# Multiplying node states in pairs with seven half products in a three-layer GNN kernel

## What is computed

```python
def first_block(x, Ws_self, Ws_neigh, bs, src, dst):
    deg = segment_sum(ones, dst, n); inv_deg = 1 / clip(deg, 1)
    h = x
    for l in range(3):
        neigh = segment_sum(h[src], dst, n) * inv_deg
        h = h @ Ws_self[l] + neigh @ Ws_neigh[l] + bs[l]
        if l != 2:
            h = relu(h)
    return h
x = layernorm(x + first_block(x, ...))
x = layernorm(x + messages(x, ...))       # 25 tiles of gathered messages
```

## Time and profile before

| | |
|---|---|
| device time, median of 3 executions | 1868.69 us (1867.55 to 1871.56) |
| span of the profiled execution | 1942.4 us |
| first aggregate starts | 227 us |
| first state of layer 1 multiplied (k = 2) | 252 us |
| y of the last aggregate | 1466 us |

### The profile page before, as it was taken

How to read it: one execution, slowest core, us unless ns; L and a number is a source line. 1 busy time by engine, 2 the same in 40 slices (tenths; PEclk the granted TensorE clock), 3 DMA queues, 4 the chain that set the end, 5 groups by cost and what they waited for, 6 DMA issues and landing times.

```text
span 1942.4 us, 23120 instructions
## 1 busy us (share of the span) xinstructions
PE 1847.2 (95%) x7910; PEld 1133.5 (58%) x7910; DVE 1175.3 (61%) x1955; ACT 623.7 (32%) x1432; POOL 1137.9 (59%) x1087
## 2 busy tenths in 40 slices
PE   8999999999999989999999999999997699999987
PEld 4455555554555545555555556666665477777765
DVE  6866778677444433444344436555535489899977
ACT  1566532332000000000000000111115478788875
POOL 4400000364888877888788822777776667677770
PEclk9999999999999989999999999999998799999998
DMA  5365665433555344544444443566644234344340
GB/s 163 123 210 174 222 206 180 128 102 95 142 145 139 105 128 116 145 124 132 108 132 124 121 130 128 197 210 198 209 157 117 71 96 114 105 109 114 110 109 26
DMA packets 239540, 265.35 MB, mean 137 GB/s; under 512 B 130757, under 2 KB 176527, under 8 KB 239420
## 3 DMA queue, kind: packets, MB, share of 16 engines
q1 hardware_dynamic: 204028, 205.79, 34.7%
q0 software_dynamic: 34480, 57.58, 10.9%
q10 hardware_dynamic: 912, 0.46, 0.1%
HBM read 174.44 MB, written 89.27 MB: 136 GB/s over the span
## 4 chain that ended last, share of the span: by engine, by line
PE 70%; DVE 11%; issue 6%; ACT 4%; another core or an unknown queue 3%; POOL 3%; DMA 2%; SPq 0%; DVEq 0%; POOLq 0%; ACTq 0%
PE low L1228 37%; PE mid L1054 23%; PE low L1258 3%; PE top L1085 2%; DVE table L2023 1%; PE mid L1239 1%; ACT table L1491 1%; DVE sort L1831 1%; PE mid L1069 1%; DVE table L2026 1%; POOL sort L900 1%; POOL table L922 1%; DVE table L2040 1%; DVE wbuf L2002 1%
## 5 line engine op out<-in xcount | busy, mean ns | idle before, releaser
L1228 PE MATMUL low<-table,abuf 125*125 125x512 f16 x3750 | 844.0, 382 | 7.3 <-issue 7.2
L1228 PEld LDWEIGHTS low<-table,abuf 125*125 125x125 bf16 x3750 | 508.3, 137 | 315.2 <-issue 43.4
L1054 PE MATMUL mid<-wbuf,h_t 128*125 128x512 f32 x1200 | 556.5, 601 | 5.8 <-DVE st_out L1759 5.1
L917 POOL DMA_INDIRECT by_src<-scat_row,sort x416 | 487.1, 1171 | 126.1 <-issue 120.8
L922 POOL DMA_INDIRECT table<-msg_table,wbuf x270 | 294.3, 1090 | 128.3 <-issue 85.2
L1054 PEld LDWEIGHTS mid<-wbuf,h_t 128*125 128x125 f32 x1200 | 215.4, 189 | 217.3 <-issue 202.5
L1769 DVE SCALAR_TENSOR_TENSOR y<-low,inv_deg,st_in 125x512 f32<-125x512 f32 x75 | 56.1, 749 | 462.1 <-PE low L1228 309.7
L1713 DVE TENSOR_TENSOR abuf<-abuf,row_scale 125x750 bf16<-125x750 bf16 (+6 forms) x156 | 265.9, 1719 | 0.8
L949 POOL DMA_INDIRECT sort<-msg_table,sort x180 | 193.2, 1073 | 92.2 <-issue 54.5
L1258 PE MATMUL low<-table,wbuf 128*125 128x256 f32 x900 | 212.7, 387 | 18.1 <-ACT table L1491 11.2
L900 POOL TENSOR_TENSOR sort<-sort 128x416 f32<-128x416 f32 x26 | 31.9, 1226 | 320.7 <-DVE sort L1831 320.7
(11 more groups left out here) (245 smaller groups left out, 1595.8 us busy)
## 6 DMA issues: line engine op xcount, KB each, us to landing
abuf<-adj SPq DMA_DIRECT2D x75, 781.2 KB
adj<-table SPq DMA_DIRECT2D x25, 781.2 KB, 4.6
states<-st_out SPq DMA_DIRECT2D x75, 256.0 KB
st_in<-states SPq DMA_DIRECT2D x75, 256.0 KB
flips<-y_flip SPq DMA_DIRECT2D x48, 256.0 KB
h_t<-flips SPq DMA_DIRECT2D x192, 64.0 KB
early_rows<-sort POOLq DMA_DIRECT2D x35, 320.0 KB
table<-early_rows SPq DMA_DIRECT2D x24, 448.0 KB
```

Of the source, the lines that this page charges most:

```text
L917: pool.indirect_dma_start(out=by_src, out_offset=bass.IndirectOffsetOnAxis(ap=place_i[:, k * PIECE + j:k * PIECE + j + 1], axis=0), in_=sc ...
L1054: last = pe.matmul(to[0:TN, :], h_t[i % 2][:, k, 0:TN], weights[l % 2][:, a, k, :], start=k == 0, stop=k == KC - 1)
L1228: last = pe.matmul(p_agg[k % 2][0:TN, :], a_tile[k % 3][:, a, :], table[ps % 2][0:TN, a, h, :], start=a == 0 and h == 0, stop=a == TILES - ...
```

## The change

In layers one and two the first 22 states of a layer (`PAIRED`) are multiplied two at a time. State r (even tile) and q = r + 1 are stacked as a 2x2 matrix of half blocks (upper and lower 256 features), the two weight matrices as another, and the product is made of seven half products in place of eight; a half product is two matmuls. For that DVE forms sums and differences of the weights once a layer (`mix_weights`, in k = 1 and k = 26, into the other weight buffer), of the states once a pair (`mix_states`), and puts the half products together (`unmix_*`). A pair is begun in an odd k of layer one (four half products at a == 6) and ended in the next (three at a == 2); in layer two it is begun in an even k. `mix_states` stands at the end of DVE's work of the aggregate before the pair is begun. States 47 to 49 and 72 to 74 are multiplied as before. `h_t` has four buffers, and all four banks of `p_mid` hold half products. Because `mix_weights` needs the other weight buffer, the weights of layer 2 are loaded in k = 25. Two scratch tiles of the sort move into another buffer, so ACT's bin masks wait for `s_count` (the end of `bin_starts`) in place of `s_tot`.

```diff
+    def pair_begun(k):
+        r = k + PAIRED
+        return [r] if k < 2 * TILES and 3 <= k % TILES <= PAIRED + 1 and k % TILES % 2 else []
+    def pair_ended(k):
+        return pair_begun(k - 1) if k else []
...
-                if k == 2:
-                    sp.wait_ge(s_ps, TILES)
+                if k == TILES:
+                    sp.wait_ge(s_pn, TILES + PAIRED)
+                    sp.wait_ge(s_ps, TILES + PAIRED)
                     for a in range(2):
                         load_weights(2, a)
...
+            def pair_first(r):
+                q, l, n = r + 1, r // TILES, pair_number(r)
...
+                pe.wait_ge(s_row, r)
+                pair_product(p_pair[0], h_t[q % HT][:, 0:HALF, :], upper).then_inc(s_half, 1)
+                pe.wait_ge(s_mixed, 1 + n + 1)
+                wm = weights[(l + 1) % 2]
+                pair_product(p_pair[1], mixed[:, 1, :, :], wm[:, 0, HALF:KC, :]).then_inc(s_half, 1)
+                pe.wait_ge(s_own, r)
+                pair_product(p_pair[2], mixed[:, 0, :, :], wm[:, 0, 0:HALF, :]).then_inc(s_half, 1)
+                pair_product(p_pair[3], h_t[r % HT][:, 0:HALF, :], wm[:, 1, 0:HALF, :]).then_inc(s_ps, 1)
+            def pair_second(r):
...
+                pe.wait_ge(s_own, r + 1)
+                pair_product(p_pair[3], h_t[r % HT][:, HALF:KC, :], wm[:, 1, HALF:KC, :], False).then_inc(s_pn, 1)
+                pair_product(p_pair[0], h_t[q % HT][:, HALF:KC, :], w[:, 0, HALF:KC, :], False).then_inc(s_pn, 1)
+                pair_product(p_pair[2], mixed[:, 2, :, :], w[:, 1, HALF:KC, :], False).then_inc(s_ps, 1)
...
+            def copy_first(r):
...
+                act.activation(st_out[(r + 1) % 2][0:TN, :], p_pair[0][0:TN, :], ACT.Copy).then_inc(s_half, 1)
...
+            def mix_weights(l):
...
+                ch.link(dve.tensor_tensor(to[:, 0, 0:HALF, :], w[:, 1, 0:HALF, :], w[:, 0, 0:HALF, :], ALU.subtract))
+                ch.link(dve.tensor_tensor(to[:, 0, HALF:KC, :], w[:, 1, HALF:KC, :], to[:, 0, 0:HALF, :], ALU.subtract))
+                dve.tensor_tensor(to[:, 1, 0:HALF, :], w[:, 1, HALF:KC, :], w[:, 1, 0:HALF, :], ALU.subtract)
+                dve.tensor_tensor(to[:, 1, HALF:KC, :], w[:, 0, HALF:KC, :], to[:, 0, HALF:KC, :], ALU.subtract).then_inc(s_wmix, 1)
+            def mix_states(r):
...
+                ch.link(dve.tensor_tensor(s1, upper_r, lower_r, ALU.add))
+                dve.tensor_tensor(upper_r, upper_q, upper_r, ALU.subtract)
+                ch.link(dve.tensor_tensor(s2, s1, upper_q, ALU.subtract))
+                dve.tensor_tensor(s4, lower_q, s2, ALU.subtract).then_inc(s_mixed, 1)
+            def unmix_first(r):
...
+                ch.link(dve.tensor_tensor(common, common, p_pair[1][0:TN, :], ALU.add))
...
+                dve.tensor_tensor(p_pair[2][0:TN, :], p_pair[2][0:TN, :], bias[0:TN, r // TILES, :], ALU.add)
...
+                ch.link(dve.tensor_tensor(st_out[r % 2][0:TN, :], common, p_pair[3][0:TN, :], ALU.add))
+                dve.tensor_tensor(st_out[r % 2][0:TN, :], st_out[r % 2][0:TN, :], p_pair[2][0:TN, :], ALU.add).then_inc(s_own, 1)
+            def unmix_rows(r):
...
+                ch.link(dve.tensor_tensor(p_pair[3][0:TN, :], st_out[(r + 1) % 2][0:TN, :], p_pair[3][0:TN, :], ALU.add))
+            def unmix_second(q):
...
+                dve.tensor_tensor(st_out[q % 2][0:TN, :], st_out[q % 2][0:TN, :], p_pair[2][0:TN, :], ALU.add).then_inc(s_own, 1)
...
+                for one in pair_begun(k):
+                    unmix_first(one)
+                for one in pair_ended(k):
+                    unmix_rows(one)
+                    for i in (one, one + 1):
+                        row_scales(i)
+                        row_lo(i)
+                    unmix_second(one + 1)
...
+                if k in (1, TILES + 1):
+                    mix_weights(k // TILES + 1)
...
+                for one in pair_begun(k + 1):
+                    mix_states(one)
```

More of the change, by code:

```diff
@@ L144, in gnn_kernel @@
     y_flip = sb("y_flip", [P, D])
-    h_t = [sb(f"h_t{b}", [P, KC, P]) for b in range(2)]
+    h_t = [sb(f"h_t{b}", [P, KC, P]) for b in range(HT)]
+    mixed = sb("mixed", [P, 3, KC // 2, TN])
+    deg_row = mixed[0:TILES, 0, 0, :]
     row_max = sb("row_max", [P, 1])
@@ L312, in gnn_kernel @@
     p_s = p_mid[:, 3 * D:4 * D]
+    p_pair = [p_mid[:, b * D:(b + 1) * D] for b in range(4)]
     p_b = [p_top[:, 0:D], p_top[:, D:2 * D]]
@@ L517, in made_at, with paired, pair_ended_last, pair_number @@
         return [n for n in (i - 1,) if by_dma(n)] + [n for n in (i,) if TILES <= n < AGGS and not by_dma(n)]
+    def paired(i):
+        return TILES <= i < AGGS and i % TILES < PAIRED
+    def pair_begun(k):
[3 more added lines that the diff above has]
+        return pair_begun(k - 1) if k else []
+    def pair_ended_last(k):
+        return bool(pair_ended(k)) and first_tile(k + 1)
+    def pair_number(r):
+        l, t = divmod(r, TILES)
+        return (l - 1) * (PAIRED // 2) + t // 2
+    def rows_bank(i):
+        if paired(i):
+            return p_pair[3] if i % TILES % 2 == 0 else p_pair[0]
+        return p_n[i % 2]
+    def singles_at(k):
+        return [i for i in made_at(k) if not paired(i)]
+    def stored_at(k):
+        return pair_begun(k) + [r + 1 for r in pair_ended(k)] + singles_at(k)
     def flips_loaded(n):
@@ L782, in _ @@
                 if not first_tile(k):
-                    for i in made_at(k):
+                    for i in stored_at(k):
                         store_state(i)
@@ L1194, in _ @@
                 for a in range(TILES):
-                    for state in made_at(k):
+                    for r in pair_ended(k):
+                        if a == 2:
+                            pair_second(r)
+                    for r in pair_begun(k):
+                        if a == 6:
+                            pair_first(r)
+                    for state in singles_at(k):
                         if a == 6 and not by_dma(state):
                             transpose_y(state)
-                        if a == (2 if by_dma(state) else 12):
+                        if a == (12 if not by_dma(state) else 2 if first_tile(k) else 14):
                             product(state, 0)
@@ L1444, in _ @@
                 bin_masks(bins_first(k))
-                for state in made_at(k):
+                for r in pair_begun(k):
+                    copy_first(r)
+                for r in pair_ended(k):
+                    row_hi(r)
+                    row_hi(r + 1)
+                for state in singles_at(k):
                     if not by_dma(state):
@@ L1939, in _ @@
                     one_hot_rows(builder_of(TILES + k + 1))
-                if k + 1 < AGGS:
+                if k + 1 < AGGS and not pair_ended_last(k):
                     scale(k + 1, 0)
```

85 lines of the change are left out of this document (61 added, 24 removed).

## The result

The changed kernel is slower: 1878.76 us median (1878.13 to 1881.31, 4 runs) against 1868.78 us (1867.55 to 1871.56, 4 runs), ratio 1.0053, 95% interval [1.0039, 1.0067]. That is +10.0 us where -2.2 were forecast. That it lies inside is luck: the part that was given 0.48, 1862 to 1872, missed, and the cause is not one that the sum held.

The account below looks back on a forecast made before the run. PE bounds k = 14 to 49, DVE's chain k = 1 to 13. Terms +16.7 - 1.7 - 18.9 + 1.7 = -2.2 us give 1868.7 - 2.2 = 1866.5 us; range 1853 to 1879.

Parts of the forecast that it names:

- the part that was given 0.48: Whole kernel: the forecast itself, a time of 1862 to 1872 us, with chance 0.48.
- PE's saving: Each pair on PE: 14 matmuls in place of 16, 1.72 us; 37.8 us for 22 pairs if nothing else waits.
- Prices of DVE's instructions: DVE's added work: `unmix_first` 2.64 us, four sums of `mix_states` 1.66 us, `mix_weights` 4.8 us.
- y of k = 13 at 498.1: DVE's chain in k = 1 to 13: grows by 15.4 us, from 482.73 to 498.1 us.
- passes 3, 4, 5: -0.7, +5.1, -0.9: DVE's stretches from y of k-1 to y of k, for k = 3, 4, 5: changes in us.
- k = 15 at 513.2: PE ends aggregate 14 at 513.2 us, against 496.5 before: 16.7 us late.
- The load that is moved: Layer 2's weights going out in k = 25 cost 0 to 5 us; 1.7 taken together with the clock.
- rival 2: Loads of k = 25 too late for `mix_weights`: aggregate 28 waits, clock falls, +4.4 us, 1873; chance 0.16.
- Rival 3: POOL's scatter becomes the bound, up to 21 us late against 17 us of room: +6 us, 1875; chance 0.09.
- The sum along PE: PE's path: +16.7 up to aggregate 14's end, -1.7 layer one, -18.9 layer two, +1.7 moved load and clock: -2.2 us.
- Rival 3's own price: During POOL's scatter: 16 `mix_states` of 1.66 us hold POOL as well, ending it up to 26.6 us later.

Follow-up runs that it names:

- e7: The changed kernel with DVE's sums of layer one done on one column instead of all: 1859.5 us, ratio 0.9945.
- e9: The changed kernel with ACT's copy of a pair's first half product in k = 3 and 5 behind the second of seven evictions: 1874.9 us, ratio 1.0027.
- e10: The changed kernel with layer two's weights loaded one aggregate sooner, in k = 24: 1880.7 us, ratio 1.0055.
- clean trace: A second trace of the unchanged kernel, no edit: span 1866.0 us, time 1867.85 us.

## Why the prediction was wrong, step by step

- **PE's saving** (1.72 us a pair, 17.66 and 15.95 in turn): right to 0.01 us.
- **Prices of DVE's instructions**: right. `unmix_first` took 2.65 us (2.64), `mix_states` 1.57 (1.66), `mix_weights` 4.83 (4.8).
- **y of k = 13 at 498.1**: it came at 501.55. The mechanism holds (e7), PE's wait in k = 13 was 9.25 us (some 9); those of k = 4 to 12 came to between 0 (k = 7 and 8) and 4.5 us, 1.8 in the mean (some 3), and part of them, in k = 4 and 5, was for blocks. The term that failed is "passes 3, 4, 5: -0.7, +5.1, -0.9": they came to +2.1, +5.0 and +1.9. DVE waits 2.70 and 2.48 us in 3 and 5 for ACT's copy. The prediction costed what DVE gets and never followed ACT, where the copy stands behind seven evictions. e9 measured it: 4.6 us at y(13), 3.8 us of time.
- **k = 15 at 513.2**: 518.57. Beside these 3.5 us, eight instructions of k = 14 ran partly at half clock (5.39 us for some 3.4), on the path; the prediction had 0 to 3.3 for that.
- **The load that is moved**, 0 to 5 us, 1.7 taken: aggregate 28 lost 7.3 us, as rival 2 describes (5.67 of wait, the rest clock). But it was not what decided: e10 took it away and the time stayed.
- **POOL**. This is the step that failed: the sum put the later start of the scatter at nothing. Rival 3 counted from the earlier trace rows: a scatter whose last piece goes out at 1125, 22.75 us ahead of the state that releases POOL, and a reader 17 us behind the indices. That room belonged to the one execution: 13 us of crawl at k = 26 and 8 us of collision at k = 51 on PE's side, and a scatter that took 645 us against 658 to 661 in all other traces. The clean trace has 1.8 us of it. A scatter that starts 15.4 us later then ends at 1156. Behind its end the first gather takes some 30 us in the traces of after (29.8) and e9 (30.0); in the clean trace of before it is 39.2, so this term could not have been read from before. With it the first gather is 6 us later than before, 1875. e9 is the test: y(13) 15.2 us later than before, and 1874.9 us. So with every other term right the sign would still have been wrong. That rival 3 named 1875 is in part luck: its condition was the hold by `mix_states`, below, which is small.
- **The sum along PE**, from the traces: counted from the start of aggregate 0, which lies 0.7 us later in after: +22.4 at k = 15 (16.7), -1.7 to k = 25 (-1.7), -18.9 in layer two (-18.9), +7.3 at k = 28 less 2.0 us for a wait of before's at k = 27 that went (together 1.7), +1.8 at k = 51 to 53 (0), +1.4 behind the first gather (0): +10.3 against -2.2.
- **Rival 3's own price**, that `mix_states` holds POOL up by 1.66 us for each pair: it holds it up, but hardly. 32 scatters of after lie beside a sum of `mix_states`; the longest takes 1.22 us, the mean 1.04 against 0.97 without, 2 us in all. Beside the scaling (L1798) 35 of 67 take over 2.5 us, one 4.18 (the 34 of the prediction, 3.0 to 4.2 us there, are 2.7 to 4.2 in its trace). The whole scatter takes 660 us with and without the sums. A scatter under the scaling, POOL and DVE:

```profile
639.98 3.58 POOL L955 DMA_INDIRECT by_src<-scat_row,sort  x1 [0.30 <-issue]
```

```profile
639.33 3.37 DVE L1798 TENSOR_TENSOR abuf<-abuf,row_scale 125x3125 bf16<-125x3125 bf16 x1
```

The Trainium skill ("SBUF — State Buffer", section "Who interferes with whom") has it that a `tensor_tensor` with both inputs in SBUF leaves descriptor generation alone, and marks the reason as inferred. The trace disagrees for both kinds. The scaling's scatter above ends 0.86 us behind the scaling. All 35 stretched ones began while a scaling ran and ended 0.83 to 0.89 us behind its end; in the clean trace of before the 22 that began ahead of one took 0.95 to 1.02 us. The scatters that began 0.03 to 0.2 us into a 128x250 f32 sum took 1.10 to 1.22 us and ended 0.82 to 0.86 us behind that sum: the same hold for the same instruction, only short because the sum is over after 0.42 us. (One that began 0.02 us into a sum took 0.97.) 39 that began under a 125x512 sum with one input in PSUM (L1872, L1878, L1879, L1888) took 0.99 us in the mean. So the price of such a sum goes by its length, and rival 3's condition held in kind, not in size.

## What to carry to other kernels

Before a profiled execution is used for slack, account for every microsecond by which its span exceeds the median; if in a stretch of it PE runs in ones and twos with gaps and the transfers stop, take another trace, because such a stretch adds room to whatever engine ran on, here POOL. Follow every engine that runs beside the bound from the event that starts it to the one that waits for it, also where it is 60% busy: a chain of 660 us that starts behind the edited stretch is moved by the edit as a whole, and what the bound gains in the meantime is worth no more than the room at its end, here 1.8 us. Work shifted to another engine has to be followed through the order of each queue that it enters, the third engine's too (here ACT's copy behind the evictions).
